# One Trainium2 core, a gated state-space block and a ternary-weight FFN: the pieces of all engines in a new order, and the last two fold tiles on VectorE alone

## The reference

```python
xc = conv4(in_proj_w @ ctx);  u = silu(xc + conv_b)
dt_lo, Bm, Cm = split(x_proj_w @ u);  delta = softplus(dt_proj_w @ dt_lo + dt_proj_b)
for t in range(256):                      # per channel (256) and state (16)
    state = state * exp(delta[t] * -exp(A_log)) + delta[t] * u[t] * Bm[t]
    y[t] = sum_n(state * Cm[t]) + D * u[t]
x = x + tanh(g_xattn) * y * silu(layernorm(x))
h = layernorm(x)
inter = silu(bitlinear(h, w_gate)) * bitlinear(h, w_up)      # 8-bit tokens, ternary weights
x = x + tanh(g_ffn) * bitlinear(fwht(inter), w_down)
```

## Time and profile before

| | |
|---|---|
| median of 3 runs | 265.23 us (263.37 to 269.11) |
| the profiled execution's own time | 265.58 us |
| its span, first to last instruction | 263.8 us |
| DVE busy | 213.9 us, 81% of the span |
| ACT busy | 157.3 us, 60% |
| PE busy | 187.3 us, 71% |
| POOL busy | 147.5 us, 56% |
| mean granted TensorE clock | 0.883 of 2.4 GHz |

### The profile page before, as it was taken

One profiled execution on the slowest core, in us unless ns is written; L12 is line 12 of the kernel. 1 busy time (PEld: TensorE's weight loads), 2 busy tenths in 40 slices (PEclk: granted clock), 3 DMA queues, 4 the chain that ended last, 5 costly groups with the idle time before them and its releaser, 6 DMA issues. The chain is left out here.

```text
span 263.8 us, 3694 instructions
## 1 busy us (share of the span) xinstructions
PE 187.3 (71%) x1209; PEld 155.8 (59%) x1216; DVE 213.9 (81%) x340; ACT 157.3 (60%) x271; POOL 147.5 (56%) x213
## 2 busy tenths in 40 slices
PE   3779489895595569867667787675596768474945
PEld 2547388794494468647557666564485547342944
DVE  4489997898989499579989897998959775579872
ACT  1685996949234556994776799735748504650040
POOL 1100890999961096039999942999930399008500
PEclk9999855899779559999997999999979988989597
DMA  3891000000000000000000000000000000000001
GB/s 60 268 363 75 1 4 0 0 1 2 0 0 2 0 0 1 2 1 0 0 2 0 0 20 4 20 4 0 0 0 24 0 20 2 0 0 1 20 22 40
DMA packets 8149, 6.34 MB, mean 24 GB/s; under 512 B 2202, under 2 KB 7874, under 8 KB 8130
## 3 DMA queue, kind: packets, MB, share of 16 engines
q1 hardware_dynamic: 7154, 6.02, 7.1%
q10 hardware_dynamic: 976, 0.09, 0.3%
HBM read 5.05 MB, written 1.05 MB: 23 GB/s over the span
## 5 line engine op out<-in xcount | busy, mean ns | idle before, releaser
L1105 POOL TENSOR_SCALAR driveT<-duT,BT 128x256 f32<-128x256 f32 x120 | 62.2, 538 | 41.0 <-issue 21.3
L823 ACT ACTIVATE decay<-delta,zero_c,aneg 128x255 f32<-128x255 f32 x128 | 65.2, 589 | 1.7 <-DVE delta L1254 1.6
L1230 DVE TENSOR_TENSOR_SCAN state<-decay,BC 128x512 f32<-128x512 f32 x30 | 36.4, 1213 | 4.4 <-issue 4.3
L1272 DVE TENSOR_TENSOR prod<-state,BC 128x1024 f32<-128x1024 f32 x32 | 38.5, 1204 | 0.6 <-issue 0.6
L463 PE MATMUL PY<-id,prod 128*128 128x128 f32 x256 | 37.9, 297 | 1.4 <-DVE x L1294 1.0
L1230 DVE TENSOR_TENSOR_SCAN state<-decay,UP 128x512 f32<-128x512 f32 x30 | 35.8, 1193 | 0.0
L463 PEld LDWEIGHTS PY<-id,prod 128*128 128x128 f32 x256 | 32.8, 154 | 2.5 <-issue 1.2
L447 PE MATMUL BC<-bc,sel 96*128 96x256 bf16 x64 | 13.1, 288 | 27.4 <-DVE prod L1272 27.3
L1130 POOL TENSOR_TENSOR wnat<-wnat 128x512 f32<-128x512 f32 x18 | 22.9, 1274 | 15.9 <-DVE wnat L1352 15.2
L933 ACT COPY hT<-GP 128x1024 f32<-128x1024 f32 x8 | 8.1, 1010 | 35.0 <-PE GP L612 35.0
L407 PE MATMUL BC<-id,driveT 128*128 128x128 f32 x120 | 21.2, 305 | 10.9 <-POOL driveT L1105 10.8
(11 more groups left out here) (208 smaller groups left out, 412.7 us busy)
## 6 DMA issues: line engine op xcount, KB each, us to landing
wnat<-in_L_ffn_w_gate_dram SPq DMA_DIRECT2D x1, 1024.0 KB, 9.6
xs<-in_x_dram SPq DMA_DIRECT2D x1, 1024.0 KB, 12.0
wnat<-in_L_ffn_w_up_dram SPq DMA_DIRECT2D x1, 1024.0 KB, 11.5
wnat<-in_L_ffn_w_down_dram SPq DMA_DIRECT2D x1, 1024.0 KB, 11.3
...
```

Of the source, the lines that this page charges most:

```text
L823: last = nc.scalar.activation(decay[:, m % RING, h, n, 1:L], delta[:, b % 2, h, 1:L], ACT.Exp, bias=zero_c[:], scale=aneg[:, h, NB * j + n ...
L1105: last = nc.gpsimd.tensor_scalar(driveT[:, m % RING, c, n], duT[:, b % 2, c], BT[:, b % 2, c, NB * j + n:NB * j + n + 1], 1.0, ALU.mult, A ...
L1230: nc.vector.tensor_tensor_scan(state[:, g % STATES, h].rearrange("p n l -> p (n l)"), decay[:, g % RING, h].rearrange("p n l -> p (n l)"), ...
L1272: nc.vector.tensor_tensor(prod[:, g % RING].rearrange("p h n l -> p h (n l)"), state[:, g % STATES].rearrange("p h n l -> p h (n l)"), PC. ...
```

## The change

Every engine's loop is replaced by a written-out list of the same pieces in another order. Each piece is issued as often as before. Pieces that take their input from another engine stand further behind the piece that makes it, about one and a half steps for each hop between engines. A few examples: on DVE, `second_rstd(0)` stood behind both scans of step 10 and stands between them; `gate_times_up(0, 1)` stood before `times_C(14)` and stands before `scan(17, 0)`; `gate_times_up(2, 1)` and `result(1, 1)` stood before `times_C(30)` and stand behind `times_C(31)`. On POOL the second tile's fold of batch 2 comes after all `drives`, as before. On ACT `silu_z(1)` stood before `decays(7)` and `dt_rows(2)` before `decays(11)`; now `dt_rows(2)` comes first, `silu_z(1)` behind it, and both stand before `decays(10)`. The tail's order changes too. The shared `fold_last` is replaced by one on DVE over all columns, with its own instructions in contiguous blocks, and `inter_T(3, t)` no longer waits for POOL. `link.begin` moves into `stats2` and `softplus_tail`.

```diff
...
-        dve_fold, pool_fold_last = sem("dve_fold"), sem("pool_fold_last")
+        dve_fold = sem("dve_fold")
...
             if part == 0:
+                link.begin(eng, n - 1)
                 eng.wait_ge(act_sp, n + 1)
                 link(ops.tensor_scalar(spm[:], spe[:], 1.0, 1.0, ALU.mult, ALU.add))
...
-
-        def fold_last(t, eng, ops, cols, done):
-
-
-            eng.wait_ge(dve_mul, LC * (B - 1) + t + 1)
-            for i in range(FOLDS):
-                src, dst = ((inter, fold), (fold, inter))[i % 2]
-                src, dst = (v[:, t].rearrange("p (g s w c) -> p g s w c", s=2, w=NI >> (i + 1), c=P)[:, :, :, :, cols]
-                            for v in (src, dst))
-                ops.tensor_tensor(dst[:, :, 0], src[:, :, 0], src[:, :, 1], ALU.add)
-                ops.tensor_tensor(dst[:, :, 1], src[:, :, 0], src[:, :, 1], ALU.subtract).then_inc(done, 1)
-                if i + 1 < FOLDS:
-                    eng.wait_ge(done, FOLDS * t + i + 1)
 
...
                     pe.wait_ge(dve_fold, FOLDS * (t + 1))
-                    pe.wait_ge(pool_fold_last, FOLDS * (t + 1))
...
-            for k in range(B):
-                p, f, n = k - 2, k - 1, k + 2
-                old, new, front = p >= 0, f >= 0, n < B
...
+            drive_rows(2, 0)
+            drive_rows(2, 1)
+            gate_T(0)
+            C_rows(1)
+            dt_proj(1)
+            drive_rows(3, 0)
+            drive_rows(3, 1)
+            weight_sum()
+            accumulate(0)
+            C_rows(2)
+            drive_rows(4, 0)
+            drive_rows(4, 1)
+            in_proj(2, 0)
+            drive_rows(5, 0)
+            C_rows(3)
...
+            drive_rows(7, 0)
+            accumulate(3)
+            weight_T(2)
+            drive_rows(7, 1)
+            accumulate(4)
+            drive_rows(8, 0)
+            drive_rows(8, 1)
+            C_rows(6)
+            accumulate(5)
+            weight_T(3)
+            weight_T(4)
+            accumulate(6)
+            drive_rows(9, 0)
+            C_rows(7)
+            x_dbl(2)
+            C_rows(8)
+            drive_rows(9, 1)
+            accumulate(7)
+            accumulate(8)
+            drive_rows(10, 0)
+            C_rows(9)
+            drive_rows(10, 1)
+            drive_rows(11, 0)
+            drive_rows(11, 1)
+            dt_proj(2)
+            drive_rows(12, 0)
+            C_rows(10)
+            weight_T(5)
+            gate_T(1)
+            drive_rows(12, 1)
+            C_rows(11)
+            in_proj(3, 0)
+            in_proj(3, 1)
+            drive_rows(13, 0)
+            drive_rows(13, 1)
+            accumulate(9)
+            tokens_T(0)
+            accumulate(10)
+            gate(0, 0)
+            C_rows(12)
...
+            down(1, 0)
+            gate(2, 1)
+            C_rows(29)
+            up(2, 0)
+            drive_rows(31, 0)
+            drive_rows(31, 1)
+            accumulate(28)
+            accumulate(29)
+            C_rows(30)
+            q2_T(1, 1)
+            up(2, 1)
+            C_rows(31)
+            accumulate(30)
+            down(1, 1)
+            accumulate(31)
+            inter_T(2, 0)
+            hadamard_mm(2, 0)
+            inter_T(2, 1)
+            tokens_T(3)
+            gate(3, 0)
+            up(3, 0)
+            gate(3, 1)
+            hadamard_mm(2, 1)
+            q2_T(2, 0)
+            up(3, 1)
+            inter_T(3, 0)
+            down(2, 0)
+            hadamard_mm(3, 0)
+            q2_T(2, 1)
+            inter_T(3, 1)
+            down(2, 1)
+            hadamard_mm(3, 1)
+            q2_T(3, 0)
+            q2_T(3, 1)
+            down(3, 0)
+            down(3, 1)
...
+            gate_out(0)
+            softplus(1)
+            decays(4)
+            decays(5)
+            decays(6)
+            decays(7)
+            decays(8)
+            decays(9)
             for_silu()
-            second_norm(f)
-            scale_tokens(f)
-            inter_out(p, 1)
-            quant_down(p, 0)
-            silu_gate(f, 0)
-            quant_down(p, 1)
-            silu_gate(f, 1)
-            inter_out(f, 0)
-            inter_out(f, 1)
-            quant_down(f, 0)
-            quant_down(f, 1)
+            conv_out(2)
+            silu_u(2)
...
+            tokens_out_early(2)
+            quant_down(1, 1)
+            decays(31)
+            for_silu()
+            silu_gate(2, 0)
+            silu_gate(2, 1)
+            q2_out_early(1, 1)
+            for_exp()
+            rstd2(3)
+            inter_out(2, 0)
+            for_silu()
+            second_norm(3)
+            scale_tokens(3)
+            inter_out(2, 1)
+            silu_gate(3, 0)
+            quant_down(2, 0)
+            silu_gate(3, 1)
+            quant_down(2, 1)
+            inter_out(3, 0)
+            inter_out(3, 1)
+            quant_down(3, 0)
+            quant_down(3, 1)
 
 
...
-            fold_last(0, pool, nc.gpsimd, slice(DVE_COLS, P), pool_fold_last)
-            fold_last(1, pool, nc.gpsimd, slice(DVE_COLS, P), pool_fold_last)
+            drives(4)
+            drives(5)
+            drives(6)
+            softplus_tail(1, pool, nc.gpsimd, pool_front_link, 0)
+            softplus_tail(1, pool, nc.gpsimd, pool_front_link, 1)
+            drives(7)
...
+            fold_tile(1, 1, 2)
+            drives(29)
+            drives(30)
+            drives(31)
+            fold_tile(2, 0, 0)
+            fold_tile(2, 0, 1)
+            fold_tile(2, 0, 2)
+            fold_tile(2, 1, 0)
+            fold_tile(2, 1, 1)
+            fold_tile(2, 1, 2)
 
...
 
             def stats2(f, link):
+                link.begin(dve, f)
...
                                                op0=ALU.mult, op1=ALU.mult).then_inc(dve_mul, 1)
+
+            def fold_last(t):
+
+                dve.wait_ge(dve_mul, LC * (B - 1) + t + 1)
+                for i in range(FOLDS):
+                    src, dst = ((inter, fold), (fold, inter))[i % 2]
+                    gap = NI >> (i + 1)
+                    src, dst = (v[:, t].rearrange("p (g s w) -> p g s w", s=2, w=gap * P) for v in (src, dst))
+                    nc.vector.tensor_tensor(dst[:, :, 0, :], src[:, :, 0, :], src[:, :, 1, :], ALU.add)
+                    nc.vector.tensor_tensor(dst[:, :, 1, :], src[:, :, 0, :], src[:, :, 1, :], ALU.subtract).then_inc(dve_fold, 1)
+                    if i + 1 < FOLDS:
+                        dve.wait_ge(dve_fold, FOLDS * t + i + 1)
...
+            scan(6, 0)
+            scan(6, 1)
+            weight_round(0)
+            weight_round(1)
+            weight_out(0)
+            times_C(5)
+            weight_out(1)
+            scan(7, 0)
+            scan(7, 1)
+            weight_round(2)
+            weight_out(2)
+            times_C(6)
+            scan(8, 0)
+            scan(8, 1)
+            times_C(7)
...
+            scan(8, 0)
+            scan(8, 1)
+            times_C(7)
+            scan(9, 0)
+            scan(9, 1)
+            times_C(8)
+            residual(0)
+            weight_out(3)
+            stats2(0, dve_ln_link)
+            scan(10, 0)
+            second_rstd(0, dve_ln_link)
+            split(2)
+            scan(10, 1)
+            times_C(9)
+            scan(11, 0)
+            scan(11, 1)
+            times_C(10)
...
+            round_down(1, 1)
+            times_C(28)
+            scan(30, 0)
+            scan(30, 1)
+            result(1, 0)
+            times_C(29)
+            gate_times_up(2, 0)
+            scan(31, 0)
+            scan(31, 1)
+            times_C(30)
+            times_C(31)
+            gate_times_up(2, 1)
+            result(1, 1)
+            residual(3)
+            stats2(3, dve_ln_link)
+            second_rstd(3, dve_ln_link)
+            token_scale(3, dve_ln_link)
+            round_tokens(3)
+            tokens_out(3)
+            absmax2(2, 0)
+            round_down(2, 0)
+            gate_times_up(3, 0)
+            fold_last(0)
+            absmax2(2, 1)
+            gate_times_up(3, 1)
+            q2_out(2, 0)
+            fold_last(1)
+            result(2, 0)
+            round_down(2, 1)
+            absmax2(3, 0)
+            q2_out(2, 1)
+            round_down(3, 0)
+            result(2, 1)
+            absmax2(3, 1)
+            round_down(3, 1)
+            q2_out(3, 0)
+            q2_out(3, 1)
+            result(3, 0)
+            result(3, 1)
```

More of the change, by code:

```diff
@@ L30 @@
 FOLDS = NI.bit_length() - 1
-DVE_COLS = 88
 DT0 = 96
@@ new lines, in _ @@
+            drive_rows(6, 0)
+            drive_rows(6, 1)
+            du_T(1)
+            C_rows(5)
+            in_proj(2, 1)
+            accumulate(2)
+            weight_T(0)
+            weight_T(1)
+            drive_rows(7, 0)
[9 more added lines that the diff above has]
+            weight_T(4)
@@ new lines, in _ @@
+            accumulate(16)
+            hadamard_mm(0, 0)
+            gate_T(2)
+            drive_rows(19, 1)
+            C_rows(18)
+            drive_rows(20, 0)
```

(32 more changed lines are left out.)

579 lines of the change are left out of this document (275 added, 304 removed).

## The result

| | us | ratio to before |
|---|---|---|
| before, median of 4 | 265.08 | |
| after, median of 4 (243.69 to 245.51) | 245.26 | 0.9248 (0.9189 to 0.9308) |
| after, run again beside other kernels, median of 6 | 244.16 | 0.9206 (0.9151 to 0.9261) |
| forecast | 248.6 (241 to 261) | |

The change takes 19.8 us off. The medians hold every execution; the ratios leave out those that took some 1.5% or more longer than the fastest of their kernel, so the two can differ a little. The profiled execution of after took 243.69 us (span 241.9) and is the fastest of its four; that of before took 265.58 (263.8).

The account below looks back on a forecast made before the run. DVE was taken to bound the loop. Its busy time less moved work and stretches, plus gaps and waits, gave 154.9 us; from 40.36, with clock +4, tail 45.75 and 2.2 + 1.78 around, 249.0, median 248.6 (241 to 261).

Parts of the forecast that it names:

- DVE's waits in the loop: Loop, DVE: waits for other engines' pieces fall to 4.2 us in place of 22.3.
- DVE's busy time, loop: Loop, DVE: 152.35 us, less 1.76 moved to the tail and 1.4 of stretches.
- small gaps: Loop, DVE: gaps of a few hundredths between instructions, +1.5 us.
- The bound: Loop: a DVE program with 23.8 us of holes; another order can take away 22.3 us of waits, nothing else.
- The walk: Four engine lists followed from `scan(2)` at 40.36 us: 4.2 us of DVE waits, `times_C(31)` ending at about 192.
- TensorE's clock: Loop, PE: slow `x_dbl(2)` and `in_proj(3)` at 1.2 GHz might delay DVE; +4 us taken, ends 0 and 9.
- Rival (b): ACT's chain around `dt_rows(2)` and `decays(10)` is late, 2 to 4 us each: 257 us; chance 0.12.
- Stretched instructions: Loop, DVE: rounding pieces lengthened alongside POOL's work, about 4.4 us; 1.4 taken off, ends 4.4 off and 12 more.
- Rival (c): Loop: DVE and POOL exclude one another at the port, worst alignment of a denser loop loses 12 us: 261; chance 0.05.
- The tail: From the end of `times_C(31)` to the last result: +0.7 us, ends -0.5 and +3, so 45.75.
- All three couplings: Tail: ACT behind `absmax2(2, 1)`, PE behind `q2_out(2, 0)` and behind `round_down(2, 1)`; the fold's gain is lost there.
- The signs: Expected in the profile: `times_C(31)` ending at 195 to 200 us, loop clock 0.9 or more, tail 45 to 47.

Follow-up runs that it names:

- changed_again: The kernel after, unchanged, run again beside scan_first and pe_filler style follow-ups on the same chip: 244.16 us, 0.9206 of the kernel before.
- old_loop_new_tail: The kernel before with its loop kept, but the new tail lists and the last fold on DVE: 265.44 us, 0.9998 of the kernel before.
- old_order_rstd_first: The kernel before with one ACT piece moved, `rstd2(f)` ahead of `softplus`: 262.07 us, 0.9833 of the kernel before.
- pe_filler: The kernel after with 36 transposes of the identity, computing nothing, added on PE ahead of `drive_rows(11, 1)`: 244.61 us, 0.9203 of the kernel before.
- new_extra_act: The kernel after with two unused copies of 256 columns added on ACT behind each `decays` from 9 to 30: 253.21 us, 0.9583 of before.
- tail_reordered: The kernel after with tile 1 of batch 3 taken earlier on PE and `absmax2(3, 1)` ahead of `result(2, 1)` on DVE: 241.03 us, 0.9094 of before.
- new_order_shared_fold: The kernel after with the fold of batch 3 shared between DVE and POOL again: 243.55 us, 0.9181 of the kernel before.

## Why the prediction was right

By its steps, with what the profile of after (own time 243.69) shows:

| step | forecast | measured |
|---|---|---|
| DVE's waits in the loop | 4.2 | 5.5 (4.7 in changed_again) |
| low clock of TensorE | +4 | 1.45, in those 5.5 |
| DVE's busy time, loop | 152.35 - 1.76 - 1.4 = 149.2 | 146.0 (147.2) |
| small gaps | 1.5 | 1.9 |
| start of `scan(2, 0)` | 40.36 | 40.89 |
| end of `times_C(31)` | 195.3, with clock 199.3 | 194.35 |
| tail | 45.75 | 45.36 (44.24) |
| around the span | 2.2 + 1.78 | 2.2 + 1.8 |

- **The bound.** That the loop is a DVE program with 22 us of holes, and that another order can take these away, held: 16.55 of 22.1 us went (22.1 by the view; the prediction says 22.3). "Nothing else" did not hold, since DVE's busy time fell by 4.55 beyond the moved 1.76. old_loop_new_tail shows that the tail gave none of the gain, and old_order_rstd_first that one hole was worth its length.
- **The walk.** `times_C(3)` 0.5 forecast and 0.54 measured, `second_rstd(0)` 0.5 and 0.73, `times_C(12)` 1.2 and 1.07, `scan(14, 1)` 1.0 and 0.94, `times_C(31)` 0.6 and 0.62. `absmax2(0, 1)` had none. Missed was `times_C(10)`. These are after's waits; in changed_again only `times_C(12)` (0.35), `scan(14, 1)` (0.94) and `times_C(31)` (0.62) of the list are left, and `scan(10, 0)` is a second one missed. The sum of the waits came out more steadily than their places. The narrowest place, `C_rows(26)` behind `inter_T(1, 1)`, held in after, and was where pe_filler's lead was lost.
- **TensorE's clock** was taken for 4 us; 1.45 was there in after, 1.0 by pe_filler on the spot, and too little to measure at the end. I took `x_dbl(2)` and `in_proj(3)` for slow. `x_dbl(2)` ran at the full clock (1.03 us), and `in_proj(3)` was slow in after (4.49) and hardly in changed_again (3.70). What cost DVE time was `drive_rows(11, 1)` and `dt_proj(2)` behind PE's wait of 4.00 us, a place that I had not named. And I charged slow pieces with their full length. In pe_filler, at the full clock, PE stood idle for 0.82 and 0.71 us before `gate_T(1)` and `in_proj(3)`, waiting for ACT, so that a part of what a slow piece costs is time that PE would have waited anyway. Rival (b), ACT's chain, did not come: `dt_rows(2)` ran at 71.44 and ACT's `decays(10)` were done before `scan(10, 0)` needed them. new_extra_act shows how near it was.
- **Stretched instructions** were the term furthest off, 3.15 us: I took 1.4 off and DVE's busy time fell by 4.55 beyond the moved pieces, about all of the stretches. The three `weight_round`s of the loop fell from 5.8 to 3.6 us and the four `round_down`s from 3.9 to 2.9, most of them at the unstretched duration (three rows; the longest `round_down` took 0.81):

```profile
57.79 2.33 DVE L1533 TENSOR_SCALAR wq<-wnat 128x2048 bf16<-128x2048 f32 x2
64.61 1.29 DVE L1533 TENSOR_SCALAR wq<-wnat 128x2048 bf16<-128x2048 f32 x1
146.75 0.69 DVE L1504 TENSOR_SCALAR wq<-ctxs 128x1024 bf16<-128x1024 f32 x1
```

  With `split` (-0.5) and `weight_means` (-0.4) less `round_tokens` (+0.2) that makes 3.9; the rest of the 4.55 is in closer overlap of neighbouring records. In changed_again the three `weight_round`s took 4.6 us, and the busy time is 147.2, so these stretches too differ between executions of one kernel. The walk by itself, without any stretches, had ended at 192 us; the sum put 3.0 of them back. Rival (c), in which a denser loop meets POOL more often, fell: the loop is denser and the stretches are fewer. That where the two engines meet decides, and not how dense the loop is, is my reading. (Its 261 us also left out that the 1.4 would not come off; with that it is 262.)
- **The tail.** All three couplings were there: `inter_out(3, 0)` right behind `quant_down(2, 1)` at +26.4 (forecast 25.8), `hadamard_mm(3, 0)` at +28.2 (27.5 to 28.4), `inter_T(3, 1)` behind `q2_T(2, 1)`. The fold took 3.9 us (4.0). It began at +19.8, forecast 18.9; in changed_again, tail_reordered and new_order_shared_fold it began at +18.9 to 19.0. The last result came at +45.4 with the first `hadamard_mm(3, 0)` at 3.50 us, and at +44.2 where it took 2.46.
- **The signs.** The errors nearly all went one way: clock and waits -2.7, busy time -3.15, tail -0.4, against start +0.5 and gaps +0.4: -5.3, from 249.0 to 243.7. That is for the profiled execution, the fastest of four; the median is 245.26, 3.3 below the forecast. Two of my allowances were for things that could go wrong and did not. Of the signs, the end of `times_C(31)` fell just below its 195 to 200, and a granted clock of 0.9 or more in the loop (it was 0.93) says little, as the old loop had 0.90.
